# Two-layer cross-channel attention on one core: block loads by partition quadrant, and a second batch's x transposed by VectorE

## The reference, cut to what matters

```python
# layer 0 (rgb = x^T, geo = y^T), H = 8 heads of d = 16
def xca(q, k, v):
    attn = softmax(einsum('bhni,bhnj->bhij', q, k) * d ** -0.5)
    out = einsum('bhnd,bhde->bhne', v, attn)
    return out.transpose(0, 2, 1, 3).reshape(b, n, c)
res_p2r = xca(heads(rgb, wq_rgb), heads(geo, wk_point), heads(geo, wv_point)) @ proj_p2r.T
res_r2p = xca(heads(geo, wq_point), heads(rgb, wk_rgb), heads(rgb, wv_rgb)) @ proj_r2p.T
x1 = (rgb + res_p2r)^T + (geo + res_r2p)^T
# layer 1: q, k from y, v from x1; scores over positions, softmax over channels of a head
o = Wo @ (softmax(q k^T / sqrt(128)) v) + bo + x1
result = (o - mean(o)) * rsqrt(var(o) + 1e-5) * gn_w + gn_b      # mean and var over the batch
```

## Time and profile before

| | us |
|---|---|
| three runs | 351.64, 349.2, 351.15 |
| median | 351.15 |
| profiled execution, its own time | 351.63 |
| its span | 349.7 |
| TensorE busy in the span | 335.8 (96%) |
| VectorE busy | 230.7 (66%) |
| ScalarE busy | 251.5 (72%) |
| GpSimd busy | 188.9 (54%) |

### The profile page before, as it was taken

The page is one execution under the profiler, slowest core; times in us unless marked ns, Lnnn a source line. Parts: engine busy times, 40 slices in busy tenths (PEclk is TensorE's granted clock), DMA queues, the critical chain, the costliest instruction groups (busy, mean ns, idle before and its releaser), DMA issues.

```text
span 349.7 us, 8291 instructions
## 1 busy us (share of the span) xinstructions
PE 335.8 (96%) x2678; PEld 281.5 (80%) x2678; DVE 230.7 (66%) x649; ACT 251.5 (72%) x410; POOL 188.9 (54%) x277
## 2 busy tenths in 40 slices
PE   6999999999999999999999999999999999999980
PEld 3788888797888889788888979888887988887760
DVE  2365694848668494866759485675948576692864
ACT  2546787778778787778878777887878787786332
POOL 0673892754819184572919467390937639092010
PEclk9899999999999999999999999999999999999995
DMA  7937566566575746556585656648575661203014
GB/s 232 382 119 243 178 201 186 205 214 236 179 275 180 274 148 219 201 189 255 180 275 177 247 174 192 254 146 272 180 221 185 199 242 49 120 0 122 0 43 200
DMA packets 29643, 66.39 MB, mean 190 GB/s; under 512 B 2368, under 2 KB 16960, under 8 KB 29632
## 3 DMA queue, kind: packets, MB, share of 16 engines
q1 hardware_dynamic: 25600, 51.57, 45.6%
q10 hardware_dynamic: 4032, 14.68, 10.7%
HBM read 49.47 MB, written 16.78 MB: 189 GB/s over the span
## 4 chain that ended last, share of the span: by engine, by line
PE 92%; DVE 3%; issue 2%; DMA 1%; ACT 1%; SPq 0%; POOLq 0%; POOL 0%
PE gacc L359 33%; PE oacc L379 9%; PE oacc L384 8%; PE oacc L380 8%; PE tpx L316 7%; PE mid L469 4%; PE mid L403 4%; PE mid L446 4%; PE mid L455 2%; PE mid L406 2%; PE mid L456 2%; DMA raw<-in_ctx 1%; PE mid L458 1%; PE mid L457 1%; PE mid L416 1%
## 5 line engine op out<-in xcount | busy, mean ns | idle before, releaser
L1013 POOL TENSOR_TENSOR xy_lo<-raw,xy_hi 128x256 fp32r<-128x256 f32 x256 | 177.8, 733 | 128.3 <-ACT xy_hi L631 128.3
L359 PE MATMUL gacc<-t 128*128 128x257 f32 x512 | 126.2, 389 | 0.8 <-ACT t L563 0.8
L359 PEld LDWEIGHTS gacc<-t 128*128 128x128 f32 x512 | 93.4, 192 | 14.8 <-issue 2.6
L631 ACT ACTIVATE xy_hi<-raw 128x1024 fp32r<-128x1024 f32 x64 | 67.1, 1051 | 0.0
L783 DVE STREAM_TRANSPOSE t<-y_blocks 128x512 f32<-128x512 f32 x56 | 64.5, 1152 | 0.0
L379 PE MATMUL oacc<-xy_hi,pq_hi 128*128 128x512 f32 x124 | 51.9, 419 | 0.4 <-ACT pq_hi L610 0.2
L380 PE MATMUL oacc<-xy_lo,pq_hi 128*128 128x512 f32 x124 | 48.9, 395 | 0.0
L563 ACT ACTIVATE t<-tpx 128x512 f32<-128x512 f32 x64 | 38.0, 597 | 9.3 <-PE tpx L329 8.4
L638 ACT ACTIVATE res<-oacc 128x512 f32<-128x512 f32 x60 | 35.7, 595 | 11.6 <-PE oacc L384 9.9
L794 DVE BATCH_NORM_STATS2 hstat<-res 128x6 f32<-128x512 f32 x60 | 39.4, 676 | 6.2 <-ACT res L638 6.2
L384 PE MATMUL oacc<-xy_hi,pq_lo 128*128 128x512 f32 x124 | 39.0, 395 | 0.0
(11 more groups left out here) (116 smaller groups left out, 427.3 us busy)
## 6 DMA issues: line engine op xcount, KB each, us to landing
raw<-in_x SPq DMA_DIRECT2D x31, 512.0 KB, 7.8
raw<-in_ctx SPq DMA_DIRECT2D x31, 512.0 KB, 9.4
y_blocks<-in_ctx SPq DMA_DIRECT2D x112, 128.0 KB
out<-res ACTq DMA_DIRECT2D x28, 512.0 KB, 6.4
out<-res SPq DMA_DIRECT2D x4, 512.0 KB, 2.6
wt<-in_weights SPq DMA_DIRECT2D x1, 896.0 KB, 6.8
raw<-in_x SPq DMA_DIRECT2D x2, 256.0 KB, 4.1
raw<-in_ctx SPq DMA_DIRECT2D x2, 256.0 KB, 5.2
```

Source lines behind the costliest of these rows:

```text
L359: mm = pe.matmul(gacc[:, 0:2 * C + 1], t[slot][:, c, C:2 * C], t[slot][:, c, :], start=(c == 0), stop=(c == CH - 1))
L631: act.activation(xy_hi[slot][:, s, :], raw[slot][:, s, :], ACT.Copy).then_inc(split_hi, 1)
L1013: piece = pool.tensor_tensor(xy_lo[slot][:, s, cols], raw[slot][:, s, cols], xy_hi[slot][:, s, cols].bitcast(f32), ALU.subtract)
```

## The change

1. **Block loads by quadrant.** `load_blocks` still issues four DMAs of 128 KB per batch, and `y_blocks` holds the same data, but one DMA now fills all four places of the 32 partitions of one quadrant a, with 128 pieces of 1 KB as before.
2. **x of the second batch of each pair in blocks.** For b = 1 the steps of the loop no longer transpose x on TensorE: new tiles `x_blocks[0]`, `x_blocks[1]` are filled by `load_x_blocks` (four DMAs of 128 KB, in addition to the whole load of x, which the split still needs), and VectorE transposes them (`x_transpose` in the vector block, two instructions of 128 x 512 per step). TensorE's `x_transpose(h, u, 1, 0)` and `(h, u, 1, 1)`, four transposes each, and ScalarE's `xt_out(h, u, 1, 0)` and `(h, u, 1, 1)` go. The batches with b = 0 and the two first steps stay as they were.
3. **Order on VectorE.** The two new transposes stand behind the two y transposes of batch b = 0; the y transposes of b = 1 move back, the first behind `partition_moments`, the second behind `c_out`.
4. **Order on SP.** The new block loads stand behind the x load of b = 1 and, in the loop, behind a wait for VectorE's second x transpose; in the two first steps behind the y load.
5. The semaphores `x_transposed` and `xt_ready` become one per b, and their counts follow.

```diff
             def load_blocks(h, n):
-                blocks = y[4 * h + n].rearrange("(i c) (a m) -> i a c m", c=W32, a=QUADS)
-                for i in range(QUADS):
-                    sp.dma_start(y_blocks[n][:, i, :], blocks[i]).then_inc(blocks_in[n], 16)
+                blocks = y[4 * h + n].rearrange("(i c) (a m) -> a c i m", c=W32, a=QUADS)
+                for a in range(QUADS):
+                    sp.dma_start(y_blocks[n][W32 * a:W32 * (a + 1), :, :], blocks[a]).then_inc(blocks_in[n], 16)
+
+            def load_x_blocks(h, u):
+
+                blocks = x[4 * h + 2 * u + 1].rearrange("(i c) (a m) -> a c i m", c=W32, a=QUADS)
+                for a in range(QUADS):
+                    sp.dma_start(x_blocks[u][W32 * a:W32 * (a + 1), :, :], blocks[a]).then_inc(x_blocks_in[u], 16)
...
-                sp.wait_ge(x_transposed, 2 * n + 2)
+                if first or b == 0:
+                    sp.wait_ge(x_transposed[b], 2 * (2 * h + u) + 2)
                 load_x(h + 1, 2 * u + b)
                 if first:
                     sp.wait_ge(y_early_done, 2 * n + 2)
                     load_y(h + 1, 2 * u + b)
+                    if b == 1:
+                        load_x_blocks(h + 1, u)
                     if u == 1:
                         load_blocks(h + 1, 2 * u + b)
                 else:
+                    if b == 1:
+                        sp.wait_ge(xt_ready[1], 2 * (2 * h + u) + 2)
+                        load_x_blocks(h + 1, u)
                     sp.wait_ge(yt_ready, 2 * n + 2)
```

TensorE's `step`:

```diff
                 elif front:
-                    x_transpose(h, u, 0, 0)
-                    x_transpose(h, u, 0, 1)
+                    x_transpose(h, u, 0)
+                    x_transpose(h, u, 1)
...
-                    x_transpose(h, u, 1, 0)
                     gram_chunks(h, u, 0, 0, 3)
                     z_operands(p - 1)
                     gram_chunks(h, u, 0, 3, 4)
                     z_products(p - 1)
                     gram_chunks(h, u, 0, 4, 8)
-                    x_transpose(h, u, 1, 1)
                     group_moments(p - 2)
```

ScalarE's `step`:

```diff
                     out_to_sbuf(h - 1, u, 1, 1)
-                    xt_out(h, u, 1, 0)
                     split_high(h, u, 1, 0, back)
                     z_out(p - 1)
                     gram_out(p, 0)
-                    xt_out(h, u, 1, 1)
```

VectorE's new function, and the top of its `step`:

```diff
+            def x_transpose(h, u, i):
+
+                n = 4 * h + 2 * u + 1
+                if i == 0:
+                    dve.wait_ge(x_blocks_in[u], 16 * QUADS * h)
+                    dve.wait_ge(gram_done, n - TB + 1)
+                blocks = x_blocks[u][:, :, :].rearrange("p i (c m) -> p m i c", c=W32)
+                dst = t[2 * u + 1][:, HC * i:HC * (i + 1), 0:C].rearrange("p m (i c) -> p m i c", c=W32)
+                dve.transpose(dst, blocks[:, HC * i:HC * (i + 1)]).then_inc(xt_ready[1], 1)
...
                     y_transpose(h, u, 0, 0)
+                    x_transpose(h, u, 0)
                     u3_out(p - 1)
                     y_transpose(h, u, 0, 1)
+                    x_transpose(h, u, 1)
```

More of the change, by code:

```diff
@@ L74, in cross_attention_pair_kernel @@
         y_blocks = [sb(f"y_blocks{n}", [C, QUADS, N // QUADS]) for n in range(4)]
+        x_blocks = [sb(f"x_blocks{n}", [C, QUADS, N // QUADS]) for n in range(2)]
         xy_hi = [sb(f"xy_hi{n}", [C, 2, N], f32r) for n in range(4)]
@@ L130, in cross_attention_pair_kernel @@
         blocks_in = [sem(f"blocks_in{n}") for n in range(4)]
+        x_blocks_in = [sem(f"x_blocks_in{n}") for n in range(2)]
         x_half_in = [sem(f"x_half_in{n}") for n in range(2)]
@@ L137, in cross_attention_pair_kernel @@
         ones_set = sem("ones_set")
-        x_transposed = sem("x_transposed")
+        x_transposed = [sem(f"x_transposed{n}") for n in range(2)]
         y_early_done = sem("y_early_done")
-        xt_ready = sem("xt_ready")
+        xt_ready = [sem(f"xt_ready{n}") for n in range(2)]
         yt_ready = sem("yt_ready")
@@ L305, in _ @@
             pe.wait_ge(ones_set, TB)
-            def x_transpose(h, u, b, i):
-                slot = 2 * u + b
-                n = 2 * (4 * h + slot) + i
+            def x_transpose(h, u, i):
+                p = 2 * h + u
                 if i == 0:
-                    pe.wait_ge(x_in[slot], 16 * (h + 1))
-                pe.wait_ge(xt_ready, n - 1)
-                chunks = raw[slot][:, 0, :].rearrange("c (r m) -> c m r", m=CH)
+                    pe.wait_ge(x_in[2 * u], 16 * (h + 1))
+                pe.wait_ge(xt_ready[0], 2 * p - 1 + i)
+                chunks = raw[2 * u][:, 0, :].rearrange("c (r m) -> c m r", m=CH)
                 for c in range(HC):
                     mm = pe.transpose(tpx[i][:, c, :], chunks[:, HC * i + c], ident)
-                mm.then_inc(x_transposed, 1)
+                mm.then_inc(x_transposed[0], 1)
             def x_transpose_early(n, i):
@@ L325, in x_transpose_early @@
                 if n > 0:
-                    pe.wait_ge(xt_ready, 2 * n - 1 + i)
+                    pe.wait_ge(xt_ready[(n - 1) % 2], 2 * ((n - 1) // 2) + 1 + i)
                 for c in range(HC):
@@ L329, in x_transpose_early @@
                     mm = pe.transpose(tpx[i][:, c, :], raw[n][:, 0, cols], ident)
-                mm.then_inc(x_transposed, 1)
+                mm.then_inc(x_transposed[n % 2], 1)
             def y_transpose_early(n, i):
@@ L350, in gram_chunks @@
                 if begin == 0 and end == CH:
-                    pe.wait_ge(xt_ready, 2 * n + 2)
+                    pe.wait_ge(xt_ready[b], 2 * (2 * h + u) + 2)
                     pe.wait_ge(yt_ready, 2 * n + 2)
                 elif begin % HC == 0:
-                    pe.wait_ge(xt_ready, 2 * n + begin // HC + 1)
+                    pe.wait_ge(xt_ready[b], 2 * (2 * h + u) + begin // HC + 1)
                     pe.wait_ge(yt_ready, 2 * n + begin // HC + 1)
@@ L559, in xt_out @@
                 n = 4 * h + slot
-                act.wait_ge(x_transposed, 2 * n + i + 1)
+                act.wait_ge(x_transposed[b], 2 * (2 * h + u) + i + 1)
                 if i == 0 and not (isinstance(n, int) and n < TB):
@@ L563, in xt_out @@
                 act.activation(t[slot][:, HC * i:HC * (i + 1), 0:C], tpx[i][:, :, :], ACT.Copy)\
-                    .then_inc(xt_ready, 1)
+                    .then_inc(xt_ready[b], 1)
             def keys_times_sums(p):
@@ L955, in step @@
                     softmax_out(p - 1)
-                    y_transpose(h, u, 1, 0)
                     half_stats(h - 1, u, 1, 0)
@@ L960, in step @@
                     partition_moments(p - 2, u)
-                    y_transpose(h, u, 1, 1)
+                    y_transpose(h, u, 1, 0)
                     variance(p - 2, u)
@@ L965, in step @@
                     c_out(p - 1, 1 - u)
+                    y_transpose(h, u, 1, 1)
                     pq_low(p - 1, 1 - u)
```

1 line of the change is left out of this document (added).

## The result

| | before | after |
|---|---|---|
| median of the runs, us | 351.14 (4 runs, 349.2 to 351.64) | 337.28 (4 runs, 336.78 to 338.05) |
| profiled execution, us | 351.63 | 336.78 |
| ratio to before, 95% interval | | 0.9636 (0.9609 to 0.9664) |
| 14 loop steps, from the first `u_products` of one to the next, us | 282.15 | 269.56 |
| one step, us | 20.15 | 19.25 |

The change makes the kernel 3.6% faster. The profiled execution lies 14.85 us under that of before: 12.59 in the loop and 2.15 ahead of it; the last 0.1 lies behind the loop or outside the span.

The account below looks back on a forecast made before the run. The prediction took TensorE's order of work to bound the loop: 351.63 us minus 12.2 for eight transposes per step gave 339.4, set at 339.5 after small stalls of 0.6 and the median's 0.5 offset; range 337.0 to 344.5.

Parts of the forecast that it names:

- the likeliest case: Whole kernel: TensorE's freed time is the gain, everything else stays covered; 339.5 us, own range 338 to 341.5, chance 0.70.
- the rival of the larger term: TensorE's dropped transposes: weight loads and switches cost more than starts show, 15.8 us; about 336 us, chance 0.05.
- TensorE bounds the step: Loop step: TensorE busy 20.18 of 20.20 us, so the order of its work is the time.
- Eight transposes are worth 0.87 us per step by the distance of starts: TensorE in the loop: two groups of four go, 0.43 and 0.44 us, 12.2 us over 14 steps.
- Stalls of 0.6 us at thin covers: TensorE's waits in the loop: small stalls of some 0.05 us per step, 0.6 us in all.
- The cover of `z`: TensorE's `m_products`, waiting for ScalarE's `z`: time in hand shrinks from 0.66 to 0.22 us, the thinnest.
- VectorE late by 0.14 at `u3_out`: VectorE at the step's start: y and x transposes of 1.15 us each end at 179.06, `u3_out` released at 178.92.
- `pq_high` stays behind the normalisation: ScalarE near the step's end: `pq_high` cannot start the full 0.87 us earlier, held by the normalisation until 175.52.
- The loads cost nothing: Block loads per step: at 400 GB/s, 4.7 MB need 12 us of a 19.3 us step, so no cost.
- Thin covers: TensorE waiting for `z` or `attn`: 0.3 us per step, 4.2 us, about 343.5 us; chance 0.14.
- Four engines: Block loads stay on four DMA engines: 24.5 us of loads per step, + 52 us, about 402 us; chance 0.05.
- VectorE as the bound: Both new VectorE transposes fully on the path: step of 21.6 us, + 20 us, about 371 us; chance 0.04.

Follow-up runs that it names:

- the last kernel: The kernel after, with half of the first batch's x also transposed on VectorE, loads and queues reordered, and `u_products` behind the first `out_half`: 331.17 us, ratio 0.9447 to before.

## Why the prediction was right, and where its sizes were off

The forecast was 339.5 us, and 337.28 lies 2.2 us under it. It lies in the stated range (337.0 to 344.5) by 0.3 us only, and outside what the likeliest case gave for itself (338 to 341.5). By the number alone the rival of the larger term (336) is nearer. What came true of the likeliest case is its mechanism: the loop lost 12.59 us where it said 12.2. The rest of the distance lies outside the loop, and that it did not carry the result out of the range is luck.

- **TensorE bounds the step: right.** The step fell by 0.90 us with TensorE idle for 0.09 us in the whole loop. That 8 transposes put back give 350.8 us again shows that nothing else in the change brings time by itself.
- **Eight transposes are worth 0.87 us per step by the distance of starts: a little small.** 0.90 was measured, 12.6 instead of 12.2 us. The other end of the term, 15.8 by busy time, was no better than its caution said: busy time counts overlaps (a group of four was 0.60 by duration and 0.43 by starts).
- **Stalls of 0.6 us at thin covers: absent.** The cover of `z` was forecast at 0.22 and is 162.91 - 162.69 = 0.22. That of `attn` was forecast at 0.49 - 0.18 = 0.31 and is 0.44. The second y transpose of the second batch was to have 0.67; it starts at 145.90 for chunks at 147.90, takes 1.10, and has 0.90.
- **VectorE late by 0.14 at `u3_out`: wrong by 0.4, on the safe side.** It waited 0.26 there. Two transposes in a row took 149.66 to 151.78, 2.12 us, not 2 x 1.15 = 2.30: their durations overlap, so the distance of starts (1.05) was the number to take, as it was on TensorE. And `pq_low` started 0.59 before TensorE's step, not 176.51 - 176.15 = 0.36. Of these 0.23, by the rows at the step's end, 0.09 are GpSimd's root, which I had held to its old time and which came 168.90 - 164.74 = 4.16 before the end of the step, not 4.07 as in the working; 0.09 are `pq_high`, which starts at 167.73 while the row of the normalisation ends at 167.82; the rest is `pq_low` following `pq_high` sooner. With the 0.18 of the transposes that is the 0.4.
- **`pq_high` stays behind the normalisation: right.** It starts at 167.73, with no wait for TensorE.
- **The loads cost nothing: right, for a smaller reason than given.** I took 400 GB/s, 12 us of work in the step. The slices read as block loads run at about 240 GB/s: 1.57 MB at 240 and 3.15 at 400 are 14.4 us. By the busy share it is 0.86 x 19.26 = 16.6 us. The sentence that went by the Trainium skill ("SBUF — State Buffer", section "Door 1: The DMA port swizzle", where 32 partitions reach 8 of 16 ports) gave 15.8 us. The rate fits with that rule, at 0.6 instead of half of the 400; the time does not depend on it, since 16.6 is still under 19.3. The experiments that gave DMA more to do, at a share of 0.91 and 0.92, show that the room was real.
- **The rivals.** Thin covers: not met, but one more VectorE instruction meets it (0.16 per step). Four engines: not met, and its mechanism is right for the old form, at 420.6 us where it gave 402. VectorE as the bound: not met. It was priced with the full transposes on the path, and the experiment shows how it would set in: first through `attn`, at a fraction of what is added. Larger term: not met, though its number is the nearest; the loop gave 12.6, not 15.8.
- **The sum.** 351.63 - 12.59 = 339.04. That the profiled execution shows 336.78 comes from its opening, 2.15 us shorter than that of the other. The change does touch the opening (its block loads are issued faster), but three other kernels here have the same opening, that with the eight unread transposes, that with the third block transpose and that with the old y order, and their profiled executions came to the loop at 36.68, 35.60 and 36.20, where after came at 34.91 and before at 37.06. The kernel before with quadrant loads came at 36.22. So much of the 2.15 belongs to the single executions, and how much of it to the change is not resolved. The prediction took its sum from one execution and shifted it by next to nothing to the median, which is right only if both medians have an opening like that execution's. The medians differ by 13.86, 1.3 more than the loop gives; the interval of the ratio is about 1 us to either side, so most of that is not resolved, and its cause stays open.

## What to carry to other kernels

Where one engine is busy without a gap, an edit is worth the distance of starts that it takes from that engine (here 0.90 us of 20.15 per step, 12.6 in the loop); then ask of each engine that takes the work over what it hands on, to whom, and how long before it is wanted. A load's shape can be worth nothing alone and everything in company: measure it with the change that needs it. When work is moved in an engine's queue, look at what the moved instruction waits for: two copies taken ahead of the normalisations in ScalarE's queue, with their waits, cost 8.6 us here.

## What the runs showed that I had not expected

**With quadrant loads the DMA engines read as busy at a little over half of their rate.** A share of 0.9 reads like a full queue, at 240 GB/s. Other slices of the same steps reach 400 to 438 at the same share. So the share alone doesn't tell what is left: the last kernel moved 272 GB/s where after moved 242, with 0.91 for 0.86 (and the quadrants in the order 0, 2, 1, 3). The page's median time of a 512 KB x load from issue to landing fell from 7.8 to 4.4 us.

**The opening runs in two ways.** In before's profiled execution, TensorE stood idle for 1.46 us for the first load of ctx, and shortly after the granted clock fell, with Gram matmuls of 3.33 us for eight. In that of after the idle time was 0.39, and the same eight took 1.90. First before, then after; PE timeline and window:

```profile
6.70 0.66 PE L343 MATMUL oacc<-cst,raw 128*128 128x128 f32 x4 [1.46 <-DMA raw<-in_ctx]
...
8.75 3.33 PE L359 MATMUL gacc<-t 128*128 128x257 f32 x8
...
8.00:12.00 4.00, 4.00 (x14) 3.33 (x14) 0.84 (x2) 1.54 (x2) 2.27 (x4) 0.57 1.04 400
```

```profile
7.95 1.90 PE L372 MATMUL gacc<-t 128*128 128x257 f32 x8
...
8.00:12.00 4.00, 4.00 (x25) 3.47 (x24) 1.38 (x2) 2.56 (x4) 2.83 (x5) 1.00 1.03 396
```

It is not the gap alone: in three of the experiments gaps of 1.07, 1.23 and 1.36 us came before a granted clock of 1.00 in the same stretch, and in another gaps of 0.64 and 0.90 us before a fall to 0.57. In the first three, groups of four transposes that begin between 4.3 and 9.1 us took 1.06 to 1.12 us, against 0.66 in before between 6.7 and 8 us, while the row still shows a clock of 1.00. Two such groups stand in after, too (at 4.19 and 5.64). So most openings have a slow part of some microseconds, at different places, and what sets it was not settled. Between the two profiled executions the wait for ctx and this part made most of the 2.15 us, so a sum taken from one profiled execution can be off by that much in the opening alone.
